# Attention and spectral block on one core: a q load moved ahead, small loads moved from POOL to SP, zero passes ahead of a transpose, and w2's preparation moved out of LN2's gap

## What is computed

```python
h = layernorm(x) * g1 + b1            # then padded and cut into windows
q, k, v = split(h @ qkv_w + qkv_b)
bias = rel_h[..., :, None] + rel_w[..., None, :]      # from q and the two tables
o = softmax(q k^T * SCALE + bias) v
x1 = x + (o @ proj_w + proj_b)
m = gelu((layernorm(x1) * g2 + b2) @ fc1_w + fc1_b)
y = x1 + m @ fc2_w + fc2_b

X, Xn = dht(y), flipped(y)            # dht: real plus imaginary part of fftn
o1k  = relu(0.5*(X w1[0] - Xn w1[1] + X w1[1] + Xn w1[0]) + b1[0])
o1nk = relu(0.5*(Xn w1[0] - X w1[1] + Xn w1[1] + X w1[0]) + b1[1])
o2k  = 0.5*(o1k w2[0] - o1nk w2[1] + o1k w2[1] + o1nk w2[0]) + b2[0]
o2nk = 0.5*(o1nk w2[0] - o2k w2[1] + o1nk w2[1] + o2k w2[0]) + b2[1]
s = softshrink(o2k + o2nk, 0.01)
out = dht(s) / s.size + y
```

## Time and profile before

| what | value |
|---|---|
| median of 3 timed runs | 196.87 us (196.72 to 197.48) |
| the profiled execution's own time | 194.18 us |
| its span | 192.4 us |
| mean granted clock of TensorE | 0.973 |
| PE busy, share of the span | 92% |
| PE weight loads | 80% |
| DVE, ACT, POOL busy | 60%, 46%, 38% |
| HBM read and written | 6.75 MB and 1.57 MB |

### The profile page before, as it was taken

The page is one execution under the profiler, slowest core; times in us unless marked ns, Lnnn a source line. Parts: engine busy times, 40 slices in busy tenths (PEclk is TensorE's granted clock), DMA queues, the critical chain, the costliest instruction groups (busy, mean ns, idle before and its releaser), DMA issues.

```text
span 192.4 us, 4149 instructions
## 1 busy us (share of the span) xinstructions
PE 177.2 (92%) x1494; PEld 154.9 (80%) x1494; DVE 114.9 (60%) x303; ACT 88.5 (46%) x231; POOL 73.9 (38%) x131
## 2 busy tenths in 40 slices
PE   7999999994969997899998999999999989999892
PEld 7866996793959876787876997788999989789892
DVE  6728785599847886678945655720021365679632
ACT  3495545752446876687885103464200124072210
POOL 1624449927366999635998020740000000000000
PEclk9999999998587999999999999999999999999999
DMA  5691237965854698957044000000011260000015
GB/s 158 173 245 24 90 96 219 217 170 173 204 158 117 189 216 198 209 125 224 12 147 137 30 0 3 0 0 0 0 44 41 82 157 9 2 0 3 0 29 134
DMA packets 9741, 19.41 MB, mean 101 GB/s; under 512 B 2301, under 2 KB 6415, under 8 KB 9722
## 3 DMA queue, kind: packets, MB, share of 16 engines
q0 software_dynamic: 3936, 11.45, 22.6%
q1 hardware_dynamic: 5050, 7.24, 14.5%
q10 hardware_dynamic: 736, 0.46, 0.9%
HBM read 6.75 MB, written 1.57 MB: 43 GB/s over the span
## 4 chain that ended last, share of the span: by engine, by line
PE 72%; DMA 8%; DVE 8%; ACT 4%; issue 2%; POOL 2%; SPq 1%; POOLq 0%; ACTq 0%; DVEq 0%
PE bank L1628 9%; PE bank L1645 8%; DMA qop<-arena 6%; PE bank L1394 6%; PE bank L1462 5%; PE bank L1663 4%; PE bank L1476 4%; PE bank L1434 3%; PE bank L1380 3%; PE bank L1369 3%; PE bank L1578 3%; PE bank L1655 3%; DMA xt<-in_x_tok 2%; PE bank L1714 2%; PE bank L1701 2%
## 5 line engine op out<-in xcount | busy, mean ns | idle before, releaser
L1178 DVE TENSOR_REDUCE negmax<-bank 98x2 f32<-98x392 f32 (+1 forms) x72 | 35.0, 525 | 10.1 <-PE bank L1434 9.4
L1462 PE MATMUL bank<-qop,kop 128*98 128x196 f32 (+4 forms) x140 | 23.7, 273 | 0.1
L937 ACT ACTIVATE arena<-bank 98x392 f32<-98x392 f32 x48 | 21.5, 491 | 3.4 <-PE bank L1462 2.5
L1434 PE MATMUL bank<-kop,qop 126*98 126x196 f32 x80 | 17.2, 306 | 5.2 <-DMA qop<-arena 4.1
L1462 PEld LDWEIGHTS bank<-qop,kop 128*98 128x98 f32 (+4 forms) x140 | 20.1, 187 | 0.9 <-issue 0.6
L1628 PE MATMUL bank<-h2t,wf 96*128 96x512 f32 x72 | 17.4, 399 | 0.4 <-ACT h2t L966 0.4
L1434 PEld LDWEIGHTS bank<-kop,qop 126*98 126x98 f32 x80 | 11.7, 185 | 7.4 <-issue 3.9
L1628 PEld LDWEIGHTS bank<-h2t,wf 96*128 96x128 f32 x72 | 13.3, 188 | 3.9 <-issue 0.6
L1645 PE MATMUL bank<-wf,arena 128*128 128x192 f32 x96 | 15.8, 326 | 0.0
L1645 PEld LDWEIGHTS bank<-wf,arena 128*128 128x128 f32 x96 | 15.7, 190 | 0.1
L1263 DVE TENSOR_TENSOR arena<-bank,arena 128x384 f32<-128x384 f32 x4 | 2.2, 557 | 22.2 <-PE bank L1645 22.2
(11 more groups left out here) (182 smaller groups left out, 392.8 us busy)
## 6 DMA issues: line engine op xcount, KB each, us to landing
kop<-arena POOLq DMA_DIRECT2D x20, 173.0 KB, 3.7
qop<-arena POOLq DMA_DIRECT2D x10, 227.5 KB, 5.2
qop<-arena SPq DMA_DIRECT2D x10, 130.0 KB, 3.7
qop<-arena POOLq DMA_DIRECT2D x10, 130.0 KB, 3.9
arena<-in_relw SPq DMA_DIRECT2D x2, 441.0 KB, 5.1
xt<-in_x_tok SPq DMA_DIRECT2D x4, 192.0 KB, 3.6
scratch<-arena SPq DMA_DIRECT2D x4, 192.0 KB, 2.0
k_last<-arena POOLq DMA_DIRECT2D x4, 173.0 KB, 3.6
```

The source lines that it names most:

```text
L937: nc.scalar.activation(pg[:, e], src[0:HWIN, 0:2 * WIN], ACT.Exp, scale=HD ** -0.5).then_inc(emptied(key), 1)
L1178: nc.vector.tensor_reduce(negmax[0:rows, n % 2, at:at + cols], ps(key)[0:rows, 0:cols * width].rearrange("p (t k) -> p t k", t=cols), AX.X ...
L1434: ins = mm(ps(key)[0:HWIN, WIN * t:WIN * t + WIN], qo(h)[0:126, c0:c0 + HWIN], ko(h)[0:126, WIN * u:WIN * u + WIN], start=True, stop=True)
L1462: ins = mm(ps(key)[0:rows, at:at + n], ko(h)[:, c0:c0 + rows], rhs, start=True, stop=True)
```

## The change

- SP issues q of head 4 right behind q of head 3, after the maxima of head 0.
- The small loads are issued by SP, three behind the maxima of each of the heads 2 to 7. There are 17 now: the host also gives w2 with its last two axes exchanged (`w2_oi`), and two loads bring it into the new tile `w2o`.
- PE passes six zero products (12 passes) into the bank of the second maxima before it waits for them.
- w2T with its transposes and the ACT copy is gone. POOL makes `w2t` from `w2o`: two sums beside the old ones (ahead of the tables' loads) and two products behind bsum, before LN2's `rstd`.
- b2w stands on PE after the outputs of bp 2, and its addition on DVE before the residuals.
- w2p stands on PE between fa and fb, and its two additions on DVE there too.
- f1c stands right behind the projection and has 40 columns for each of its six parts, not 80.
- The banks from oT on are given out in the new order.

```diff
     rotate([("wT", 1), ("eT", 0, 2), ("eT", 1, 2)])
-    rotate([("oT", f, bp) for bp in (2, 0, 1) for f in range(2)])
+    rotate([("oT", f, 2) for f in range(2)] + ["b2w"])
+    rotate([("oT", f, bp) for bp in range(2) for f in range(2)])
     rotate([("pr", n) for n in range(4)])
-    rotate(["w2T", "b2w", "w2p", "f1c"])
+    rotate(["f1c"])
...
-    rotate([("fb", n) for n in range(4)])
+    rotate(["w2p"] + [("fb", n) for n in range(4)])
...
@@ SP @@
             for h in range(NH):
                 load_maxima(h)
-                if h < 2:
-                    load_q(OWN - 2 + h)
+                if h == 0:
+                    load_q(OWN - 2)
+                    load_q(OWN - 1)
+                if 2 <= h < 8:
+                    for dst, src in later_inputs[3 * (h - 2):3 * (h - 2) + 3]:
+                        sp.dma_start(dst, src, allow_slow_non_contiguous=True).then_inc(late_in, 16)
                 if h == 1:
...
@@ POOL @@
-                    (w12[:, 1, 1], a["w2"][1].rearrange("(f n) i o -> (n i) f o", f=2)))
+                    (w12[:, 1, 1], a["w2"][1].rearrange("(f n) i o -> (n i) f o", f=2)),
+                    (w2o[:, 0], a["w2_oi"][0].rearrange("(f n) o i -> (n o) f i", f=2)),
+                    (w2o[:, 1], a["w2_oi"][1].rearrange("(f n) o i -> (n o) f i", f=2)))
...
-                    if OWN <= h < 2 * OWN:
-                        for dst, src in later_inputs[3 * (h - OWN):3 * (h - OWN) + 3]:
-                            pool.dma_start(dst, src, allow_slow_non_contiguous=True).then_inc(late_in, 16)
                     if h + 1 < OWN:
                         load_k(h + 1)
...
             nc.gpsimd.tensor_tensor(wps[:], wbd[:, 1, 0], wbd[:, 1, 1], ALU.add).then_inc(wps_done, 1)
+            nc.gpsimd.tensor_tensor(wsum[:, 0], w2o[:, 0], w2o[:, 1], ALU.add).then_inc(wsum_done, 1)
+            nc.gpsimd.tensor_tensor(wsum[:, 1], w2o[:, 0], w2o[:, 1], ALU.subtract).then_inc(wsum_done, 1)
...
             nc.gpsimd.tensor_tensor(bsum, b2r[:, 0], b2r[:, 1], ALU.add).then_inc(bsum_done, 1)
+            pool.wait_ge(wsum_done, 4)
+            for x in range(2):
+                nc.gpsimd.tensor_tensor(
+                    w2t[:, x].rearrange("p f (n i) -> p f n i", n=NB // 2),
+                    wsum[:, x, :, None].to_broadcast([CF, 2, NB // 2, BS]),
+                    half4[:, None, :, None].to_broadcast([CF, 2, NB // 2, BS]), ALU.mult).then_inc(w2t_done, 1)
...
@@ ACT @@
-            act.wait_ge(*is_full("w2T"))
-            nc.scalar.copy(w2t.rearrange("p x f c -> p (x f c)"), ps("w2T")[0:CF, 0:4 * CF]).then_inc(emptied("w2T"), 1)
...
@@ DVE @@
             for bp in (2, 0, 1):
                 outputs_read(dve, nc.vector.tensor_copy, 1, bp)
+            dve.wait_ge(*is_full("b2w"))
+            dve.wait_ge(bsum_done, 1)
+            nc.vector.tensor_tensor(bs, ps("b2w")[:, 0:C], bsum, ALU.add).then_inc(emptied("b2w"), 1)
             dve.wait_ge(xpb_done, NT)
...
@@ PE @@
                 pe.wait_ge(*is_free(key))
+                if h == 1:
+                    kept_busy(6, ps(key))
                 pe.wait_ge(max_split, h + 1)
...
             for bp in (2, 0, 1):
+                if bp == 0:
+                    pe.wait_ge(wbd_done, 4)
+                    pe.wait_ge(late_in, 17 * 16)
+                    pe.wait_ge(*is_free("b2w"))
+                    for f in range(2):
+                        ins = mm(ps("b2w")[:, CF * f:CF * f + CF], b20c[:, f:f + 1].to_broadcast([CF, 128]),
+                                 wbd[:, 1, 1, f], start=True, stop=True)
+                    ins.then_inc(filled("b2w"), 1)
...
-                    ins = mm(ps("f1c")[:, 80 * m:80 * m + 80], wf1_f32[:, c, 128 * m:128 * m + 128],
-                             ln2[:, c, 1:2].to_broadcast([CF, 80]), start=c == 0, stop=c == 1)
+                    ins = mm(ps("f1c")[:, 40 * m:40 * m + 40], wf1_f32[:, c, 128 * m:128 * m + 128],
+                             ln2[:, c, 1:2].to_broadcast([CF, 40]), start=c == 0, stop=c == 1)
```

More of the change, by code:

```diff
@@ L728, in _ @@
                 pool.wait_ge(k_loaded[h % NOK], 32 * (h // NOK + 1))
-            pool.wait_ge(late_in, 15 * 16)
+            pool.wait_ge(late_in, 17 * 16)
             for c in range(2):
@@ L957, in _ @@
                 outputs_read(act, nc.scalar.copy, 0, bp)
-            act.wait_ge(*is_full("w2T"))
-            nc.scalar.copy(w2t.rearrange("p x f c -> p (x f c)"), ps("w2T")[0:CF, 0:4 * CF]).then_inc(emptied("w2T"), 1)
-            act.wait_ge(late_in, 15 * 16)
+            act.wait_ge(late_in, 17 * 16)
             def h2_high_part(bp):
@@ L1237, in _ @@
             residual(3)
-            dve.wait_ge(late_in, 15 * 16)
+            dve.wait_ge(late_in, 17 * 16)
             dve.wait_ge(*is_full("f1c"))
-            nc.vector.tensor_tensor(f1s[:], ps("f1c")[:, 0:480:80], f1b[:], ALU.add).then_inc(emptied("f1c"), 1)
+            nc.vector.tensor_tensor(f1s[:], ps("f1c")[:, 0:240:40], f1b[:], ALU.add).then_inc(emptied("f1c"), 1)
             h2_low_part(0)
-            dve.wait_ge(*is_full("w2p"))
-            dve.wait_ge(wps_done, 1)
-            nc.vector.tensor_tensor(wab[:, 0], ps("w2p")[0:CF, 0:2 * CF].rearrange("p (f c) -> p f c", f=2),
-                                    wbd[:, 1, 0], ALU.add)
-            nc.vector.tensor_tensor(wab[:, 1], ps("w2p")[0:CF, 2 * CF:4 * CF].rearrange("p (f c) -> p f c", f=2),
-                                    wps[:], ALU.add).then_inc(emptied("w2p"), 1)
-            dve.wait_ge(*is_full("b2w"))
-            dve.wait_ge(bsum_done, 1)
-            nc.vector.tensor_tensor(bs, ps("b2w")[:, 0:C], bsum, ALU.add).then_inc(emptied("b2w"), 1)
             for n in range(2, 4):
@@ L1332, in _, with kept_busy @@
             mm = nc.tensor.matmul
-            def kept_busy(passes):
+            def kept_busy(passes, into=bank[7]):
                 for _ in range(passes):
-                    mm(bank[7][:, 0:128], zeros[:], zeros[:], start=True, stop=True)
+                    mm(into[:, 0:128], zeros[:], zeros[:], start=True, stop=True)
             pe.wait_ge(zeros_set, 1)
@@ L1567, in _ @@
                     ins.then_inc(filled(key), 1)
-            pe.wait_ge(late_in, 15 * 16)
+            pe.wait_ge(late_in, 17 * 16)
             pe.wait_ge(weights_in, 32)
@@ L1580, in _ @@
                 ins.then_inc(filled(key), 1)
-            pe.wait_ge(wbd_done, 4)
-            pe.wait_ge(*is_free("w2T"))
-            for i in range(4):
-                ins = nc.tensor.transpose(ps("w2T")[0:CF, CF * i:CF * i + CF], wbd[:, 1, i // 2, i % 2],
-                                          ident[0:CF, 0:CF])
-            ins.then_inc(filled("w2T"), 1)
-            pe.wait_ge(*is_free("b2w"))
-            for f in range(2):
-                ins = mm(ps("b2w")[:, CF * f:CF * f + CF], b20c[:, f:f + 1].to_broadcast([CF, 128]), wbd[:, 1, 1, f],
-                         start=True, stop=True)
-            ins.then_inc(filled("b2w"), 1)
-            pe.wait_ge(*is_free("w2p"))
-            pe.wait_ge(*is_read("w2T"))
-            for i in range(4):
-                ins = mm(ps("w2p")[0:CF, CF * i:CF * i + CF], w2t[:, i // 2, i % 2], wbd[:, 1, 1, i % 2],
-                         start=True, stop=True)
-            ins.then_inc(filled("w2p"), 1)
             pe.wait_ge(wf1_again, 32)
-            pe.wait_ge(late_in, 15 * 16)
+            pe.wait_ge(late_in, 17 * 16)
             pe.wait_ge(*is_free("f1c"))
@@ L1666, in over_channels @@
                     ins.then_inc(filled(key), 1)
+            pe.wait_ge(w2t_done, 2)
+            pe.wait_ge(*is_free("w2p"))
+            for i in range(4):
+                ins = mm(ps("w2p")[0:CF, CF * i:CF * i + CF], w2t[:, i // 2, i % 2], wbd[:, 1, 1, i % 2],
+                         start=True, stop=True)
+            ins.then_inc(filled("w2p"), 1)
             in_turn = [(0, 0), (1, 0), (0, 1), (1, 1), (2, 0), (2, 1), (3, 0), (3, 1)]
```

43 lines of the change are left out of this document (26 added, 17 removed).

## The result

The changed kernel takes 191.94 us (median of 6 runs, 190.22 to 193.22). The kernel before, six runs of it by then, has a median of 196.36. The ratio is 0.9875, with the interval 0.9827 to 0.9924; some executions of a kernel are a few per cent longer than its others at a lower granted clock, and the ratio leaves these out, while the medians of all runs, which keep them, stand at 0.9775. The change makes the kernel faster, clear of the noise and inside the range given, but by 1.25% where 7.4 us, 3.8%, was forecast.

A forecast was written before the change was run, and what follows sets the result against it. The prediction took PE, on the chain for 72% of the 192.4 us span, as the bound, so its waits and half clock counted. Terms 1.45 + 1.2 + 1.4 + 1.9 + 1.87 - 0.38 = 7.4 us gave 189.4 us, range 187.1 to 193.0.

The forecast's parts named there:

- Small loads from POOL to SP: Heads 8 to 10: POOL's queue stops being the bound, shortening PE's operand waits; 1.9 us gained, bounds 0.5 to 2.6.
- rival (b): Heads 5 to 11: DMA engines bind, small loads only change queue, waits stay; 1.9 us goes, 191.3; chance 0.12.
- (c): Rival: slower, since small loads on SP's queue delay the next head's maxima; 198.5 at 1.5 us per head; chance 0.04.
- Fifth q early: Before head 4: issuing its q right behind head 3's removes PE's wait for that load; 1.45 us gained.
- Zeros: Gap before the second head's maxima: six zero passes keep the clock up; 1.2 us there, 1.4 for the second fall.
- rival (a): From 46 us the clock falls anyway despite the zeros; 1.2 + 1.4 go, 4.8 us gained, 192.0; chance 0.20.
- the second fall: Heads 4 to 11: half clock after head 4's wait, credited to the zeros; 1.4 us gained, bounds 0 and 1.8.
- w2's preparation: LN2's gap: taking w2T and its ACT copy out lets PE go on earlier; 1.87 us gained.
- w2p behind fa: Between fa and fb: 8 passes, 0.89 us, in a PE wait of 0.51 us; 0.38 us lost.
- b2w ahead of the last outputs: Last outputs: 4 passes, 0.45 us, hidden in a PE wait of 0.65 us; 0.
- Rival (d): Clock falls, waits move to other operands, and a late bsum eats LN2's gain; 196.5; chance 0.04.

The follow-up runs named there:

- e7_sponly: The kernel before with only its 15 small loads moved to SP, behind the maxima of heads 2 to 6: 194.67 us, ratio 1.0034.
- e1_pool: The changed kernel with its 17 small loads back on POOL, behind the rel loads of heads 5 to 10: 192.19 us, ratio 0.9897.
- e0_after: The changed kernel run again, nothing altered: 190.94 us, ratio 0.9862.
- e2_nozeros: The changed kernel without the six zero passes: 192.88 us, ratio 0.9895.
- e8_dummies: The changed kernel with 16 small loads packed into one early load, plus thirteen element-wise loads repeated on SP into unread tiles: 190.39 us, ratio 0.9816.
- e10_packed_only: The kernel before with only its small loads packed by the host into one array, loaded early: 190.98 us, ratio 0.9852.
- e5_q5late: The changed kernel with q of head 4 loaded behind the maxima of head 1 again: 191.32 us, ratio 0.9885.
- e14: The kernel of e16 plus the six zero passes: 189.68 us, ratio 0.9749.
- e16: The kernel before with packed small loads and the reordering behind the attention loop; q of head 4 late, no zeros: 189.29 us, ratio 0.9785.
- e15: Repeat of e9's kernel on another chip (all parts, packed loads, twelve zero products): 187.86 us, ratio 0.9689.
- e9: The changed kernel with packed small loads and six further zero products at the third head's row maxima: 187.61 us, ratio 0.9676.

## Why the prediction was right or wrong

*Small loads from POOL to SP, 1.9 us gained*: the step that failed. Its first half held: POOL's queue stopped being the clock. The second rested on the words in rival (b) that the small loads "only change queue". They do not: 15 loads that were 544 packets on POOL's queue became 3,344 on SP's (8,394 less 5,050 in e7_sponly), the share went from 0.75 to above 1, and the landing that I had set at 3.9 to 5.2 us for the rel load became 6.7: with the 3.0 us to its issue 9.7 us, where a head's load has 7.55. Alone the move measures 0 (e7_sponly), inside the full change 0.35%, which is not told from 0 (e1_pool against e0_after). The missing 3.4 us of the profiled pair lie here and more: from head 5 to head 11 1.64 us were lost where 1.9 should have been won, some 3.5 us short. Up to head 5 the gain was 3.40, about 0.4 below the terms for that part (1.45, 1.2 and 1.1 of the 1.4); behind head 11 it was 2.24 where 1.5 stood.

*Rivals (b) and (c)* are what happened, both in part. The engines fill, as in (b), by the small loads that (b) had counted as unchanged. And the maxima of (c) are late: PE waits for them 2.2 us in e7_sponly, 1.77 in e0_after, 1.49 in e2_nozeros and 1.9 in e8_dummies, and in the changed kernel's first profile the chain runs through them without a wait in the list. That is not the 1.24 us per head at which the change loses, but in e7_sponly it is more than what the operand waits grew by. Which of the two costs more was not separated. I had excused (c) since only one load has 768 pieces; I should have added up the pieces of all 17. The Trainium skill, DMA: Bandwidth & Descriptors, section SWDGE vs HWDGE vs iDMA, sends irregular transfers to GpSimd; e7_sponly agrees so far as SP was no better for them (1.0034), though not by the 198 us that I had put beside the rule, and inside the full change SP was no worse (e1_pool against e0_after). In e10_packed_only, where the host lays the small loads out as one regular one, the time is 0.9852 of before.

*Fifth q early, 1.45*: the wait went, but not by this part alone. The q load was late while three small loads of POOL's (47.66 to 49.65) stood among the transfers, and moving those ends the wait as well (53.46 in e10_packed_only); what early q adds is 0.1 us at head 4 there, some 0.4 where the clock holds (e5_q5late), and nothing in the times. The 1.45 should have stood for both parts together.

*Zeros, 1.2 and 1.4*: the gap closed to 0.39 us with PE not delayed. The clock fell all the same in the profiled execution, 2 us later, and held in others (e0_after, e5_q5late), so rival (a) is right for some executions and the forecast for others. The 1.4 us of the second fall came in full: head 4 to head 5 takes 3.45 us instead of 4.58, and head 5 without its wait 4.19 instead of 4.46. But the zeros did not bring it, since the fall is gone in e2_nozeros and e10_packed_only as well; what these share with the changed kernel is that head 4 no longer waits for its load. In the ratios the six zero products are worth 0.3% beside the pieces (e2_nozeros) and 0.4% beside packed loads (e14 against e16), both within the noise; twelve are worth 1.1%, which is clear of it. So the term of 1.2 was too high, and the 1.4 stood under the wrong part. (An odd head takes 4.16 to 4.2 us, and the packed kernels, not 4.05, so the upper bound there was 1.4 to 1.5 and not 1.8.) The reason given for taking an upper value, that VectorE had waited for PE, was sound; what was missing is that VectorE's pace leaves PE further small gaps behind the filled one (PE is busy for 0.96 of the 2 us from 46 to 48).

*w2's preparation, 1.87*: right, 1.94; f1c took 2.60 us at 40 columns against 2.67 at 80, so its time does not follow the columns, as taken. *w2p behind fa, 0.38 lost*: 0.16 up to fb's start, and nothing up to its end. *b2w ahead of the last outputs, 0*: right, the outputs' transposes (L1584) wait 0.23 us, and for VectorE. Rival (d)'s late bsum cost nothing: VectorE waited 0.31 us for it, and the first residual behind it still waited 0.45 us for PE.

What stays open: how much of the move's cost is the fuller engines and how much SP's own queue; why one execution keeps the clock and the next does not with the same instructions, and, once the clock holds and the pieces are gone, whether the loads of heads 6 and 7 are late by their bytes or by the round trip (share 0.81 in e15 with waits of 1.4 us).

## What to carry to other kernels

Before a strided load moves from one DMA queue to another, count its pieces, and compare the packets that the profile's page lists for each queue. Small loads are better laid out as one array and fetched in one piece ahead of the busy stretch, which here was worth 1.5%, 2.9 us, by itself where the change of queue was worth nothing. When two waits lie close together, ask whether one cause feeds both before both prices go into the sum. When a gap is filled to hold the clock, look at the pauses behind it as well. And a stretch of one profile is compared with that of another only where both held the same clock.

## What the runs showed of the hardware

- The queue of GpSimd carried the small loads in about one sixth of the packets that SP's did: 544 against 3,344 for the same 15 loads. On SP's queue it is one packet for each piece and 16 more for each load: the 13 dummy loads of e8_dummies have 2,976 pieces and added 3,184 packets (8,490 less 5,306).
- The packets on SP's queue, nearly all small loads, took 18 ns of an engine each on average in the changed kernel, and q0 used 19.9% of the engines per MB beside them, 16.7% without. Beside the element-wise loads alone (e8_dummies) q0 used 17.2%.
- SP's issues of small loads were longer where the engines were full: 0.42 us for one broadcast load at 53.85 (DMA share 0.17 from 52 to 54 and 0.46 from 54 to 56), 2.55 for two at 62.73 (share 1.07), while POOL's issue of the same two (b2r) took 1.14 us in e1_pool (share 0.95 from 60 to 62, 0.64 from 62 to 64).
- The granted clock fell to 0.50 behind a wait of 2.26 us in e9 and behind one of 1.84 us before; in the changed kernel waits of 1.56 and 1.55 us left it at 1.00, while behind one of 1.57 us in e14 it fell to 0.50. The length of the wait alone does not decide it.
